# A four-layer graph network on one core: the sampled search's two passes moved to one slot, GpSimd's corrections rewritten

## The reference

```
for s in range(2):
    logits = (Xa @ W1) @ W2 @ (Xa @ W3).T
    # per row: keep the largest probabilities until their sum reaches 0.9, drop the rest
    idx = argsort(-logits); csum = cumsum(softmax(sorted logits))
    k_i = sum(csum < 0.9) + 1
    A = softmax(where(rank < k_i, logits, -inf))
    Xf, Xb, Xa = Rf @ Xf, Rb @ Xb, A @ Xa
    Z += Xf @ U1[s] + Xb @ U2[s] + Xa @ U3[s]
out = layernorm(X + Z) * gamma + beta
```

## Time and profile before

| | |
|---|---|
| median of 3 runs | 3489.06 us (3486.54 to 3490.57) |
| profiled execution, its own time | 3488.64 us |
| its span | 3486.8 us |
| TensorE busy | 3144.3 us (90%) |
| VectorE | 2454.0 us (70%) |
| GpSimd | 2146.4 us (62%) |
| ScalarE | 1599.1 us (46%) |
| mean granted TensorE clock | 0.957 of full |

### The profile page before, as it was taken

How to read it: one execution, slowest core, us unless ns; L and a number is a source line. 1 busy time by engine, 2 the same in 40 slices (tenths; PEclk the granted TensorE clock), 3 DMA queues, 4 the chain that set the end, 5 groups by cost and what they waited for, 6 DMA issues and landing times. The chain is left out here.

```text
span 3486.8 us, 42119 instructions
## 1 busy us (share of the span) xinstructions
PE 3144.3 (90%) x13212; PEld 2272.6 (65%) x13212; DVE 2454.0 (70%) x3451; ACT 1599.1 (46%) x2357; POOL 2146.4 (62%) x4214
## 2 busy tenths in 40 slices
PE   4999989998699999999976698988899999996899
PEld 3788878885477777777754254544566566664788
DVE  6983410002998889888884799999978999998000
ACT  2211321225566666666653455555555655552200
POOL 1212421124788888888880677877988788886211
PEclk9999999998899999999988899999999999998899
DMA  6643444443122122112211111211222222223254
GB/s 246 223 162 132 130 147 163 163 142 86 44 58 58 58 58 66 54 59 63 65 33 62 47 52 52 62 44 56 57 81 76 73 84 82 74 83 102 91 201 172
DMA packets 140702, 327.59 MB, mean 94 GB/s; under 512 B 15456, under 2 KB 93664, under 8 KB 129248
## 3 DMA queue, kind: packets, MB, share of 16 engines
q1 hardware_dynamic: 140512, 325.30, 29.3%
HBM read 286.70 MB, written 38.54 MB: 93 GB/s over the span
## 5 line engine op out<-in xcount | busy, mean ns | idle before, releaser
L1027 ACT ACTIVATE junk<-E,negp 128x3327 uint8<-128x3327 f32 x208 | 637.3, 3064 | 142.4 <-issue 107.8
L1399 DVE SCALAR_TENSOR_TENSOR U<-E,trial 128x3327 f32<-128x3327 f32 x182 | 678.5, 3728 | 0.0
L922 PE MATMUL bank<-big,adj 128*128 128x512 f32 x1352 | 609.9, 602 | 8.7 <-ACT t L1053 8.7
L922 PEld LDWEIGHTS bank<-big,adj 128*128 128x128 f32 x1352 | 252.9, 192 | 329.2 <-issue 328.1
L294 PE MATMUL bank<-big,E 128*128 128x256 f32 x1664 | 366.2, 381 | 2.4 <-PEq L58 1.7
L882 PE MATMUL bank<-Hc,PT 128*128 128x256 f32 x1248 | 305.1, 396 | 69.2 <-ACT PT L1066 69.2
L294 PEld LDWEIGHTS bank<-big,E 128*128 128x128 f32 x1664 | 315.9, 191 | 49.3 <-issue 6.6
L882 PE MATMUL bank<-Hc,adj 128*128 128x256 f32 x1456 | 335.4, 382 | 10.7 <-ACT adj L1066 10.7
L1361 DVE TENSOR_REDUCE nmax<-E 128x1 f32<-128x3327 f32 x52 | 188.0, 3615 | 207.4 <-ACT E L1070 207.4
L882 PEld LDWEIGHTS bank<-Hc,PT 128*128 128x128 f32 x1248 | 245.9, 199 | 129.9 <-ACT PT L1066 79.7
L882 PEld LDWEIGHTS bank<-Hc,adj 128*128 128x128 f32 x1456 | 277.8, 191 | 72.9 <-issue 23.0
(11 more groups left out here) (248 smaller groups left out, 5937.2 us busy)
## 6 DMA issues: line engine op xcount, KB each, us to landing
adj<-adjT SPq DMA_DIRECT2D x131, 448.0 KB, 3.4
E<-adjT SPq DMA_DIRECT2D x32, 1664.0 KB, 6.9
adj<-adjT SPq DMA_DIRECT2D x104, 384.0 KB, 3.4
adj<-adjT SPq DMA_DIRECT2D x20, 1664.0 KB, 7.0
E<-adjT SPq DMA_DIRECT2D x26, 1216.0 KB, 5.7
xt<-xin SPq DMA_DIRECT2D x52, 128.0 KB, 5.7
x_d<-xn SPq DMA_DIRECT2D x52, 128.0 KB, 1.7
xt<-x_d SPq DMA_DIRECT2D x52, 128.0 KB, 5.2
```

The lines of the kernel that those rows point to most:

```text
L922: last = mm(agg[:, 0:w], adj[:, SPAN * (k % 2) + j - AGG[k]], rhs[:, j], start=(j == 0), stop=False)
L1027: go(junk[:, 0:N], E[:, t % DEPTH, 0:N], func, bias=negp[:, t % 2, j:j + 1], scale=1.0, accum_out=acc_[:, t % 2, j:j + 1]).then_inc(summed ...
L1399: V_.scalar_tensor_tensor(out=U[:, 0:N], in0=e, scalar=point, in1=e, op0=ALU.is_ge, op1=ALU.mult, accum_out=found))
```

## The change

- The first pass over the second point, `sums(R, 1, 0)`, moves from slot 0 to slot 1, directly ahead of `sums(R, 1, 1)`. (The passes of the first point stay in slots 2 and 3.) The four pass semaphores become one counter `summed`, and each pass waits for the pass before it.
- GpSimd keeps its numbers otherwise. `prepare` makes, ahead of the pass, p/2 and the sum's constant part, so that the error `slip` follows from `over` (one addition, as soon as the first pass is done) and `sign` (one instruction). The next point `negp` is made straight from the last one by a factor, without clamping to the bracket: five dependent steps from the second pass's end for j = 0. The bracket is done behind it. The error kept with a bracket end is now `slip` itself.
- Constants: SHIFT of the first step 1.4 to 1.2, AIM of the first step 3.0 to 2.0 (where STEER was 2.0 already), KEEP_END of the second step 0.75 to 0.85, UNDER 1 - 2^-22 to 1 - 2^-20.
- The code allows a third point; with POINTS = (2, 2) it isn't used.

The diff, without the declarations, with the removed lines of `update` left out (they are printed above):

```diff
@@ -19,18 +19,16 @@
 EVALS = (3, 4)
 MARKED = -1.0
 
-PASSES = (2, 2)
-POINTS = 2
-SHIFT = (1.4, 0.0)
-STEER = (2.0, 4.0)
-AIM = (3.0, 4.0)
-KEEP_END = (0.8, 0.75)
+POINTS = (2, 2)
+SHIFT = (1.2, 0.0)
+AIM = (2.0, 4.0)
+KEEP_END = (0.8, 0.85)
 RIDGE = (8.0, 4.0)
 QUANTILE = 1.2815515655446004
 DENSITY = 0.17549833193248685
 ROOT = 4096.0
 STRIDE = 1.5
-UNDER = 1.0 - 2.0 ** -22
+UNDER = 1.0 - 2.0 ** -20
 
 SLOTS = 4
...
@@ -707,6 +705,15 @@
             early = NT - LAG
             spread = [b for i in range(rounds + 1) for b in [last_at(i)] if b is not None and i < tiles + LATE]
             kept = len(spread)
+            passes = []
+            for i in range(rounds):
+                R, F = aim_at(i), exp_at(i)
+                if R is not None:
+passes += [(R, 1, 0), (R, 1, 1)] + [(R, 2, 1)] * (POINTS[R // NT] - 2)
+                if F is not None:
+passes += [(F, 0, 0), (F, 0, 1)]
+            tiles_with = lambda t, j: sum(POINTS[x // NT] > j for x in range(t + 1))
+            nth = {which: i + 1 for i, which in enumerate(passes)}
             turned = lambda i: sum(first(sent_at(k)) or first(post_at(k)) for k in range(i))
             dense_g = lambda i: sum(first(sent_at(k)) for k in range(i))
...
@@ -1015,17 +1022,13 @@
     go = nc.scalar.activation
 
     def sums(t, j, m):
-        if m == 0:
-            act.wait_ge(aimed[j], t + 1)
-            if j > 0:
-                act.wait_ge(summed[j - 1], PASSES[j - 1] * (t + 1))
-            elif t >= 1:
-                act.wait_ge(summed[1], 2 * t)
-        else:
-            act.wait_ge(summed[j], 2 * t + 1)
+        if m == 0 or j == 2:
+            act.wait_ge(aimed[j], tiles_with(t, j))
+        if nth[t, j, m] > 1:
+            act.wait_ge(summed, nth[t, j, m] - 1)
         func, acc_ = ((ACT.Relu, over), (ACT.Sign, sign))[m]
         go(junk[:, 0:N], E[:, t % DEPTH, 0:N], func, bias=negp[:, t % 2, j:j + 1], scale=1.0,
-           accum_out=acc_[:, t % 2, j:j + 1]).then_inc(summed[j], 1)
+           accum_out=acc_[:, t % 2, j:j + 1]).then_inc(summed, 1)
 
     for i in range(rounds):
         L, F, T, X = score_at(i), exp_at(i), turn_at(i), post_at(i)
@@ -1078,8 +1081,6 @@
             if k == 0 and Y is not None:
                 act.wait_ge(x3_done, Y + 1)
                 go(junk_x[:], x3b[:, Y % 2], ACT.Copy, accum_out=stat3[:, Y % 2, 0:1]).then_inc(ln3_a, 1)
-            if k == 0 and R is not None:
-                sums(R, 1, 0)
             if k == 1 and W is not None:
                 act.wait_ge(tp3_done, W + 1)
                 go(hT3[:, W % 2], misc[:, 0:D], ACT.Copy).then_inc(hT3_ready, 1)
@@ -1124,6 +1125,7 @@
                     act.wait_ge(y_ready, b + 1)
                     go(junk_y[:], y[:, X % 2], ACT.Copy, accum_out=stat[:, X % 2, 0:1]).then_inc(ln_a, 1)
                 if R is not None:
+                    sums(R, 1, 0)
                     sums(R, 1, 1)
             if k == 2:
                 if first(G):
...
@@ -1190,24 +1195,21 @@
         pool.sem_clear(step_done)
         n[0] = 0
 
-    def offer(t, j):
-        then(ts(negp[:, t % 2, j:j + 1], cand[:, t % 2, 0:1], -UNDER, None, ALU.mult))
-        pool.sem_inc(aimed[j], 1)
-
     def prepare(t):
         q, step = t % 2, t // NT
-        p = cand[:, q, 0:1]
-        then(ts(up[:, q, 0:2], known[:, 4 + 2 * step:6 + 2 * step], p, ga[:, q, 12:13], ALU.mult, ALU.add),
-             ts(up[:, q, 3:4], p, p, RIDGE[step] ** 2, ALU.mult, ALU.mult))
-        then(tt(up[:, q, 4:5], up[:, q, 3:4], ga[:, q, 11:12], ALU.mult))
+        up_ = lambda a: up[:, q, a:a + 1]
+        p = up_(24)
+        then(ts(up_(2), p, N / 2 + AIM[step], trial2[:, t % DEPTH, NEG:NEG + 1], ALU.mult, ALU.add),
+             ts(up[:, q, 0:2], known[:, 4 + 2 * step:6 + 2 * step], p, None, ALU.mult),
+             ts(up_(3), p, p, RIDGE[step] ** 2, ALU.mult, ALU.mult))
+        then(tt(up_(4), up_(3), ga[:, q, 11:12], ALU.mult))
 
     def guess(t):
         q, d, step = t % 2, t % DEPTH, t // NT
         ga_ = lambda a: ga[:, q, a:a + 1]
         restart()
         z, nm = Zs[:, d:d + 1], nmax[:, d:d + 1]
-        tgt, below = (trial2[:, d, a:a + 1] for a in (GOAL, BELOW))
-        p = cand[:, q, 0:1]
+        p = up[:, q, 24:25]
         pool.wait_ge(exp_done, t + 1)
         if t >= DEPTH:
             pool.wait_ge(probs_ready, t - DEPTH + 1)
@@ -1217,63 +1219,90 @@
              ts(ga_(4), ga_(2), ROOT, -ROOT - math.log(N), ALU.mult, ALU.add))
         then(ts(ga_(5), ga_(3), 1.0 / N, nm, ALU.mult, ALU.add))
         then(tt(ga_(6), ga_(4), ga_(5), ALU.subtract))
-        then(ts(ga_(7), ga_(6), 2.0, 0.01, ALU.mult, ALU.add),
-             ts(ga_(8), ga_(5), 1.0, -SHIFT[step], ALU.mult, ALU.add))
+        then(ts(ga_(7), ga_(6), 2.0, 0.01, ALU.mult, ALU.add))
         then(tt(ga_(9), ga_(7), half, ALU.pow),
-             tt(ga_(10), ga_(8), ga_(7), ALU.add))
+             tt(ga_(10), ga_(5), ga_(7), ALU.add))
         then(ts(ga_(13), ga_(9), -QUANTILE, ga_(10), ALU.mult, ALU.add))
-        then(ts(ga_(14), ga_(13), -0.001, -36.0, ALU.min, ALU.max))
-        then(tt(p, e_, ga_(14), ALU.pow))
-        offer(t, 0)
+        then(ts(ga_(14), ga_(13), SHIFT[step] - 0.001, SHIFT[step] - 36.0, ALU.min, ALU.max))
+        then(tt(ga_(8), e_, ga_(14), ALU.pow))
+        then(ts(negp[:, q, 0:1], ga_(8), -UNDER * math.exp(-SHIFT[step]), None, ALU.mult))
+        pool.sem_inc(aimed[0], 1)
         shape4 = lambda ap: ap.rearrange("p a b -> p (a b)")
         then(tt(shape4(parts[:, 0]), z.to_broadcast([P, 4]), shape4(outset[:, 0]), ALU.mult),
-             ts(tgt, z, P_NUC, None, ALU.mult),
-             ts(ga_(12), z, -P_NUC, None, ALU.mult),
+             ts(p, ga_(8), math.exp(-SHIFT[step]), None, ALU.mult),
+             tt(trial2[:, d, GOAL:NEG + 1:2], z.to_broadcast([P, 3]), known[:, 8:11], ALU.mult),
              tt(ga_(15), z, minus, ALU.pow))
         then(tt(ends2[:, d], parts[:, 0], outset[:, 1], ALU.add),
-             ts(below, tgt, 1 - 2.0 ** -24, None, ALU.mult),
+             ts(cand[:, q, 0:1], p, 1.0, None, ALU.mult),
              ts(ga_(11), ga_(15), ga_(9), 1.0 / DENSITY, ALU.mult, ALU.mult))
         prepare(t)
 
     def update(t, j):
         q, d, step = t % 2, t % DEPTH, t // NT
         up_ = lambda a: up[:, q, a:a + 1]
...
+        last = j == POINTS[step] - 1
+        p, slip, slope = up_(24), cand[:, q, 1:2], ga[:, q, 11:12]
         ends = ends2[:, d]
         lo, hi = ends2[:, d, 0, 0:1], ends2[:, d, 1, 0:1]
...
+        point = trial2[:, d, POINT:POINT + 1]
+        signs = sign[:, q, j:j + 1]
         wide = lambda ap: ap.unsqueeze(2).to_broadcast([P, 2, 2])
...
+        restart()
+        if j < 2:
+            pool.wait_ge(summed, nth[t, j, 0])
+            then(tt(up_(5), over[:, q, j:j + 1], up_(2), ALU.add))
+        pool.wait_ge(summed, nth[t, j, 1])
+        if j < 2:
+            then(ts(slip, signs, up_(0), up_(5), ALU.mult, ALU.add))
+        else:
+            then(ts(slip, signs, up_(16), up_(17), ALU.mult, ALU.add))
+        if j == 0:
+            then(ts(up_(13), slip, slope, STRIDE, ALU.mult, ALU.min))
+        else:
+            then(tt(up_(7), slip, up_(6), ALU.subtract))
+            then(ts(up_(8), up_(7), up_(7), up_(3), ALU.mult, ALU.add),
+                 ts(up_(9), up_(7), up_(10), up_(4), ALU.mult, ALU.add))
+            then(tt(up_(11), up_(8), minus, ALU.pow),
+                 tt(up_(12), up_(9), slip, ALU.mult))
+            then(ts(up_(13), up_(12), up_(11), STRIDE, ALU.mult, ALU.min))
+        then(ts(up_(14), up_(13), -STRIDE, None, ALU.max))
+        then(tt(up_(15), e_, up_(14), ALU.pow))
+        if not last:
+            then(tt(negp[:, q, j + 1:j + 2], negp[:, q, j:j + 1], up_(15), ALU.mult))
+            pool.sem_inc(aimed[j + 1], 1)
+        if j < 2:
+            then(ts(took[:, 1:2], slip, up_(1), None, ALU.is_ge),
+                 tt(up_(21), up_(15), p, ALU.mult))
+        else:
+            then(ts(up_(18), signs, up_(19), up_(20), ALU.mult, ALU.add),
+                 tt(up_(21), up_(15), p, ALU.mult))
+            then(ts(took[:, 1:2], up_(18), 0.0, None, ALU.is_ge))
+        then(ts(took[:, 0:3:2], took[:, 1:2].to_broadcast([P, 2]), -1.0, 1.0, ALU.mult, ALU.add))
+        then(tt(parts[:, 0], ends, wide(took[:, 0:2]), ALU.mult),
+             tt(parts[:, 1], cand[:, q].unsqueeze(1).to_broadcast([P, 2, 2]),
                 wide(took[:, 1:3]), ALU.mult))
...
+        then(tt(ends, parts[:, 0], parts[:, 1], ALU.add))
+        if last:
+            then(ts(point, up_(21), hi, lo, ALU.min, ALU.max))
             pool.sem_inc(bracketed, 1)
+            return
+        if j == 1:
+            then(tt(up_(22), slip, up_(1), ALU.subtract),
+                 tt(up_(23), signs, up_(0), ALU.mult),
+                 ts(up_(19), p, 0.5, None, ALU.mult),
+                 tt(up_(25), up_(21), p, ALU.add),
+                 tt(up_(26), up_(21), p, ALU.subtract),
+                 tt(slope, up_(9), up_(11), ALU.mult))
```

(47 more changed lines are left out.)

6 lines of the change are left out of this document (1 added, 5 removed).

## The result

The changed kernel takes 3549.7 us (median, 3548.6 to 3550.3) against 3488.8 for the kernel before: ratio 1.0176, 95% interval 1.0163 to 1.0189. It is slower by 61 us; the forecast was 3502, the range 3466 to 3530. The profiled execution has a span of 3547.9 us for 3486.8.

A forecast was written before the change was run, and what follows sets the result against it. GpSimd's dependent chain was taken to bound the first step, VectorE then TensorE the second. From 3488.6 us, +12 for GpSimd's corrections and +1.5 for the first tile gave 3502 us (+0.4%), range 3466 to 3530.

The forecast's parts named there:

- In the first step a further turn is nearly free: VectorE's closing loop, first step: one more turn hardly costs time, as VectorE has 35 us of work in 38.8.
- I take none, with bounds of three either way: Closing-loop turns under the new constants: no net change assumed, bounds of three turns either way, -20 to +27 us.
- GpSimd's chain as the bound of the first step: First step: GpSimd's dependent chain closes on itself once a round and sets the period, 38.8 us before.
- GpSimd's extra work: GpSimd's corrections and guess: +0.5 us a tile, +12 us over 24 first-step rounds (-5 to +29).
- The order of passes: ScalarE's first pass over the second point moved to slot 1: TensorE's 2.1 us wait should go; costed at nothing.
- the cover: TensorE work, about 6 us, before slot 2's late copy is needed; without it, up to 3.1 us a round lost.
- The first tile: Before 863 us the second correction's input comes up to one pass later, half hidden: +1.5 us, once.
- 3, "more closing turns": VectorE's closing loop: three or four more turns in the second step, +25 us more, 3527 us; chance 0.11.
- Rival 2: VectorE's closing loop: three or four turns fewer, -20 to -30 us, 3475 to 3480 us; chance 0.20.
- Rival 4: GpSimd's corrections cost the same as before, added companions hiding in gaps: 3489 to 3492 us; chance 0.15.
- rival 5: GpSimd and VectorE share bandwidth, stretching 0.5 us added to 0.9: 3511 us; counted within the forecast's 0.44.
- Rival 1: ScalarE's block in slot 0 was the bound: removing TensorE's 2.1 us a round gives 45 us, 3443; chance 0.10.

The follow-up runs named there:

- e11: The changed kernel with AIM 3 for 2 in VectorE's search of the first step only: 3488.5 us, ratio 1.0003.
- e10: The kernel before with AIM 2 for 3 alone: 3510.5 us, ratio 1.0067.
- e7: The changed kernel with SHIFT 1.1 and four more dependent one-column steps in GpSimd's guess of each first-step tile: 3521.6 us, ratio 1.0092.
- e4: The changed kernel with the first pass over the second point back in slot 0: 3549.5 us, ratio to before 1.0179.
- e3: The kernel before with the first pass over the second point in slot 1 instead of slot 0: 3482.5 us, ratio 0.9985.
- e5: The kernel before with GpSimd's two additions per first-step tile done by VectorE at the head of the next round: 3458.9 us, ratio 0.9911.
- e1: The changed kernel with SHIFT of the first step 1.1 for 1.2, nothing else: 3491.6 us, ratio to before 1.0012.
- e6: The changed kernel with SHIFT 1.1 and GpSimd's two additions per first-step tile moved to VectorE: 3453.7 us, ratio 0.9896.
- e8: The kernel before with first pass in slot 1, the two additions on VectorE, SHIFT 1.1, AIM 2, KEEP_END 0.85, old corrections: 3440.5 us, ratio 0.9857.

## Why the prediction was wrong

*The step that failed* is "In the first step a further turn is nearly free", and with it "I take none, with bounds of three either way". The turns moved by seven more in the first step and three fewer in the second, and the first sentence holds only for a turn that stands alone. The masks of tiles 10 to 13 before:

```profile
1283.72 3.61 DVE L1446 SCALAR_TENSOR_TENSOR E<-U,E 128x3327 f32<-128x3327 f32 x1
1332.80 3.61 DVE L1446 SCALAR_TENSOR_TENSOR E<-U,E 128x3327 f32<-128x3327 f32 x1
1367.66 3.60 DVE L1446 SCALAR_TENSOR_TENSOR E<-U,E 128x3327 f32<-128x3327 f32 x1
1402.53 3.60 DVE L1446 SCALAR_TENSOR_TENSOR E<-U,E 128x3327 f32<-128x3327 f32 x1
```

Tile 11 with two turns took 49.1 us and the next two 34.9 each: VectorE's floor is 34.9, the round 38.8, and it caught up. I carried that over to any number. The masks of tiles 14 to 17 after, where tile 15 has four turns:

```profile
1442.58 3.62 DVE L1477 SCALAR_TENSOR_TENSOR E<-U,E 128x3327 f32<-128x3327 f32 x1
1509.03 3.60 DVE L1477 SCALAR_TENSOR_TENSOR E<-U,E 128x3327 f32<-128x3327 f32 x1
1543.85 3.62 DVE L1477 SCALAR_TENSOR_TENSOR E<-U,E 128x3327 f32<-128x3327 f32 x1
1578.72 3.62 DVE L1477 SCALAR_TENSOR_TENSOR E<-U,E 128x3327 f32<-128x3327 f32 x1
```

Ten extra turns in three tiles are 90 us of VectorE, at 8.8 to 9.4 us each; it can give back 4.7 us in every later round (39.5 less 34.8, the round of a tile with one turn right behind them). Six of the ten rounds of tiles 15 to 24 ran at that floor and those of tiles 18 and 24 gave a part: 33 us. 90 less 33 is 57, and the stretch is 451.8 - 395 = 57 longer than ten plain rounds. The number of extra turns in the step was 3 before and 10 after, and it was their heap that cost, not the count. A loop whose turns are the worst of 128 rows has a long tail. Redoing the search's arithmetic in numpy finds one row each in tiles 15, 18 and 21 with 28, 20 and 42 values left where all others of the tile have at most 7. A turn takes eight, so 4, 3 and 6 turns, as the chip shows. In those rows the second evaluation falls far short of the goal and moves the upper end 28, 20 and 42 values off. The third just reaches the goal and moves the lower end, so the upper end stays where it is. With AIM 3 in the search the third falls two or three values short and brings the upper end in. That is not quite what I wrote before e11, where all three were to land past the goal. That these are the same rows on the chip is argued from the equal turns; the arithmetic misses a turn here and there (31 for 32 in e10).

*What held.* GpSimd's chain as the bound of the first step: 39.5 us a round; the forecast was 39.0 to 39.6. GpSimd's extra work was mis-sized a little: +0.7 us a tile for +0.5, so 17 us for 12 over the 24 rounds. The timeline of GpSimd after shows the terms:

```profile
1210.31 0.19 POOL L1253 TENSOR_TENSOR up<-over,up 128x1 f32<-128x1 f32 x1 [0.17 <-POOL up L1205]
...
1216.33 0.73 POOL L1357 TENSOR_TENSOR t<-t 128x256 f32<-128x256 f32 x1 [0.18 <-POOL trial L1286]
1217.15 4.12 POOL L1361 TENSOR_TENSOR adj<-t,Hc 128x256 f32<-128x256 f32 x1
1221.53 0.19 POOL L1253 TENSOR_TENSOR up<-over,up 128x1 f32<-128x1 f32 x1 [0.26 <-POOL adj L1361]
1221.83 0.34 POOL L1256 TENSOR_SCALAR cand<-sign,up 128x1 f32<-128x1 f32 x1
1222.27 0.30 POOL L1260 TENSOR_SCALAR up<-cand,ga 128x1 f32<-128x1 f32 x1
1222.66 0.23 POOL L1268 TENSOR_SCALAR up<-up 128x1 f32<-128x1 f32 x1
1222.96 3.85 POOL L1269 TENSOR_TENSOR up<-known,up 128x1 f32<-128x1 f32 x1
1226.90 0.19 POOL L1271 TENSOR_TENSOR negp<-negp,up 128x1 f32<-128x1 f32 x1
...
1228.11 3.65 POOL L1281 TENSOR_TENSOR parts<-ends,took 128x4 f32<-128x4 f32 x1
...
1232.30 3.77 POOL L1301 TENSOR_SCALAR cand<-up,ends 128x1 f32<-128x1 f32 x1
```

The second correction lies between 1210.31 and 1216.33, 6.0 us (forecast 5.9). The first, from line 1253 at 1221.53, has three stops in it by VectorE (lines 1269, 1281, 1301). From its start to the next round's guess at 1238.14 are 16.6 us, less 10.2 of stops 6.4, for which I had 6.2 against 5.6 before. The five steps to the new point are there, lines 1256 to 1271, and one of them is stopped for 3.3 us. Nobody's round got shorter by them.

The lock of the Trainium skill ("SBUF — State Buffer", "Who interferes with whom") held against sharing: with 1.1 us added the round of e7 is 40.6 us, and not the 41.5 of sharing.

*The order of passes* I had costed at nothing. In the changed kernel that is right (e4), alone it gives 5.5 us (e3). TensorE's wait for the turned copies was to go and hardly did (17.7 us for 20.7), and ScalarE waits for GpSimd longer than before, 116 us in the ten rounds for 50. From 2650 to 3150 us TensorE waits for no copy of ScalarE's, so the cover was there in the second step.

*The second step.* Three turns fewer gave 6 us net. The profile after has tile 27 at 40.1 us for 49.2 (one turn for two), and tile 46 at 61.2 for 51.9 with equal turns: what was won went back into waits where TensorE bounds. Every run with KEEP_END 0.85 has 42 or 43 turns there and every one with 0.75 has 45; no run changed KEEP_END by itself.

*The first tile*: I had added 1.5 us. Tile 0 was masked 8.9 us earlier (one turn for two), and with GpSimd bound this was used up by tile 9.

*The rivals.* 3, "more closing turns", named the mechanism and had the sign; its place (second step) and its size (three or four) were wrong. Rival 2, fewer turns, came true in the second step, but its three turns gave 6 us and not 20 to 30, as two of them (tiles 44 and 47) lie where TensorE bounds. Rival 4 is out by the round of 39.5 us for 38.8, rival 5 by e7. Rival 1 is refuted by e3 and e5 to e7 together.

*What would have been luck.* With SHIFT 1.1 the changed kernel takes 3491.6 us, inside the range. But the sum behind it would be another than mine: 17 us for GpSimd's work, less what fewer turns gave, which I had put at nothing. The mask of tile 25 starts 10 us later in e1 than before the change, and that of tile 51 only 6 us later.

## What to carry to other kernels

Here the engine that never waited for another was the bound, even at 87% busy (344 of 395 us), as the runs that added and removed work on it show: the gaps between its own dependent instructions are its work. Price a change there by the whole chain, by distances from start to start, not by the latency to one signal. And where a loop's turns depend on the worst row of a tile, no constant that steers it may be costed from the mean: redo the arithmetic over all tiles, take the largest count, and compare its heap with what the engine can catch up per round.

## What the runs showed of the hardware that was not expected

GpSimd's period follows its own work to a tenth of a microsecond in both directions although it is stopped for over two fifths of the round: +1.1 us of work gave +1.1 (e7), -1.7 gave -1.7 (e6). On which instruction a stop falls differs between kernels and stretches (line 1361 took 4.1 us in each of the ten plain rounds after, and 0.7 in most of tiles 15 to 24). Their sum hardly does: five stops and 16.7 to 17.2 us a round in the plain rounds before, after and in e1, e3 and e5 to e8, summed over GpSimd's timelines.
